# Image 0 in four quarters, its tables from a second queue, and unread products on TensorE ahead of the first statistics

## The reference, cut to what matters

```python
def _gn(v, G=32, eps=1e-05):
    g = v.reshape(B_, H_, W_, G, C_ // G)
    m = jnp.mean(g, axis=(1, 2, 4), keepdims=True)
    s = jnp.var(g, axis=(1, 2, 4), keepdims=True)
    return ((g - m) / jnp.sqrt(s + eps)).reshape(v.shape)

def _L0_conv_ref(x, w1, b1, w2, b2, bias_w, bias_b):
    bias = x @ bias_w.T + bias_b
    xf = jnp.fft.rfftn(x.reshape(B, H, W, 4, 96), axes=(1, 2), norm='ortho')
    xr, xi = (xf.real, xf.imag)
    r1 = relu(_block_mul(xr, w1[0]) - _block_mul(xi, w1[1]) + b1[0])
    i1 = relu(_block_mul(xr, w1[1]) + _block_mul(xi, w1[0]) + b1[1])
    r2 = _block_mul(r1, w2[0]) - _block_mul(i1, w2[1]) + b2[0]
    i2 = _block_mul(r2, w2[1]) + _block_mul(i1, w2[0]) + b2[1]
    out = jnp.fft.irfftn(complex(r2, i2), s=(H, W), axes=(1, 2), norm='ortho')
    return out.reshape(B, H, W, C) + bias

return x + _L0_conv_ref(_gn(x), ...)
```

## Time and profile before

| | us |
|---|---|
| median of 3 runs | 426.53 (425.56 to 427.38) |
| the profiled execution's own time | 424.55 |
| its span | 422.7 |
| TensorE busy | 392.5 (93%) |
| VectorE busy | 289.6 (68%) |
| ScalarE busy | 228.7 (54%) |
| mean granted TensorE clock | 0.984 |

### The profile page before, as it was taken

The page is one execution under the profiler, slowest core; times in us unless marked ns, Lnnn a source line. Parts: engine busy times, 40 slices in busy tenths (PEclk is TensorE's granted clock), DMA queues, the critical chain, the costliest instruction groups (busy, mean ns, idle before and its releaser), DMA issues.

```text
span 422.7 us, 19391 instructions
## 1 busy us (share of the span) xinstructions
PE 392.5 (93%) x8578; PEld 323.9 (77%) x8578; DVE 289.6 (68%) x728; ACT 228.7 (54%) x514; POOL 167.5 (40%) x114
## 2 busy tenths in 40 slices
PE   3369799999999999999999999999999999998996
PEld 3367689887887878788787878788787988876794
DVE  4797677874687557865678657865578747877525
ACT  2884766356752676447662667436663567426420
POOL 0000001990049600992039800793019900699200
PEclk9859999999999999999999999999999999999999
DMA  6670000180003500170002600062001800040004
GB/s 219 184 256 4 2 3 4 40 299 3 3 17 147 182 3 4 40 283 20 3 4 105 236 3 5 29 227 86 3 5 40 301 3 3 18 174 3 5 3 151
DMA packets 12407, 32.98 MB, mean 78 GB/s; under 512 B 4962, under 2 KB 6660, under 8 KB 12324
## 3 DMA queue, kind: packets, MB, share of 16 engines
q1 hardware_dynamic: 12324, 31.74, 21.2%
HBM read 16.00 MB, written 12.58 MB: 68 GB/s over the span
## 4 chain that ended last, share of the span: by engine, by line
PE 86%; ACT 5%; DVE 4%; issue 2%; DMA 1%; DVEq 0%; SPq 0%; ACTq 0%
PE bank L576 86%; DVE rho L1047 2%; DMA x_sb<-in_x 1%; ACT rho L969 1%; ACT y L930 1%; ACT junk L918 1%; ACT yraw L910 1%; ACT r L940 1%; ACT biasw L944 1%; DVE o_sb L1142 0%; ACT w2s L944 0%; DVE r L1126 0%; ACT z L950 0%; ACT junk L921 0%; DVE w1R L1047 0%
## 5 line engine op out<-in xcount | busy, mean ns | idle before, releaser
L576 PE MATMUL bank<-biasw,yt 128*64 128x384 f16 x1008 | 92.6, 327 | 0.0
L576 PE MATMUL bank<-w2s,rho 128*64 128x96 f16 x3072 | 84.9, 207 | 0.0
L882 POOL TENSOR_TENSOR x_sb<-x_sb,added 128x384 f32<-128x384 f32 x8 | 8.0, 1001 | 192.1 <-DVE yraw L1113 192.1
L576 PEld LDWEIGHTS bank<-w2s,rho 128*64 128x64 f16 x3072 | 80.0, 109 | 5.3 <-issue 2.5
L892 POOL COPY yt<-y 128x1024 f16<-128x1024 f16 x42 | 84.1, 2059 | 0.0
L884 POOL TENSOR_TENSOR x_sb<-x_sb,added 128x384 f32<-128x384 f32 x56 | 74.6, 1364 | 0.0
L576 PEld LDWEIGHTS bank<-biasw,yt 128*64 128x64 f16 x1008 | 54.0, 110 | 20.2 <-issue 0.3
L576 PE MATMUL bank<-w1R,y 128*128 128x192 f16 (+3 forms) x768 | 60.3, 228 | 5.4 <-ACT y L930 3.4
L1047 DVE SCALAR_TENSOR_TENSOR rho<-bank,rho 128x256 f16<-128x256 f32 (+2 forms) x128 | 40.2, 365 | 32.1 <-ACT rho L969 18.6
L950 ACT ACTIVATE z<-bank 128x384 f16<-128x384 f32 x72 | 35.3, 490 | 49.0 <-PE bank L576 48.1
L576 PE MATMUL bank<-tab,x_sb 128*128 128x128 f32 x384 | 50.5, 287 | 8.1 <-DMA x_sb<-in_x 6.5
(11 more groups left out here) (116 smaller groups left out, 474.6 us busy)
## 6 DMA issues: line engine op xcount, KB each, us to landing
x_sb<-in_x SPq DMA_DIRECT2D x16, 768.0 KB, 7.2
out<-o_sb SPq DMA_DIRECT2D x14, 768.0 KB, 4.0
y<-y SPq DMA_DIRECT2D x24, 128.0 KB, 2.7
out<-o_sb SPq DMA_DIRECT2D x8, 192.0 KB, 1.9
tab<-in_tab SPq DMA_DIRECT2D x1, 672.0 KB, 6.3
o_sb<-in_bias_wt SPq DMA_DIRECT2D x4, 144.0 KB, 2.8
b1raw<-in_b1h SPq DMA_DIRECT2D x1, 384.0 KB, 6.6
g<-in_w2t SPq DMA_DIRECT2D x2, 144.0 KB, 2.6
```

The source lines that it names most:

```text
L576: return nc.tensor.matmul(o, lhsT, rhs, start=start, stop=stop, **kw)
L882: nc.gpsimd.tensor_tensor(tiles[:, 0, :], tiles[:, 0, :], added[:, 0, :], ALU.add).then_inc(x_shifted, 1)
```

## The change

- SP issues x of image 0 as four transfers of two tiles each, with a semaphore each (x0_loaded), as its first instructions; the width table is issued by ACT as ACT's first instruction. p1 of image 0 waits for a quarter ahead of the matmuls that use it.
- TensorE gets three batches of products that nobody reads: b1ones as weights, and b1ones repeated four times as 512 columns, into the bank c_bank[2]. Ten stand after p1(0), behind a wait for b1ones; seven after mean(0); twelve after the w2 products, before c1.
- The high part of the first third of y of image 0 is made by DVE (first_high) instead of ACT; ACT makes the second and third.
- largest_bias moves behind the three y_low on DVE.
- The counts of x_loaded for image 2 and later even images change, as image 0 no longer counts there.

```diff
@@ SP
-            sp.dma_start(tab[:, 0:WIDTH_COLS], tab_d[:, 0:WIDTH_COLS]).then_inc(width_in, 16)
-            load(0, 0)
+            for q in range(4):
+                sp.dma_start(x_sb[0][:, 2 * q:2 * q + 2, :].rearrange("p t c -> p (t c)"),
+                             x[0, :, q * 2 * CH:(q + 1) * 2 * CH]).then_inc(x0_loaded[q], 16)
@@ TensorE, p1
-                if ct == 0:
-                    pe.wait_ge(x_loaded[p][h], (b - p) * 8 + 16)
+                if ct == 0 and not first:
+                    pe.wait_ge(x_loaded[p][h], (b - p) * 8 + 16 * p)
                 for i in range(4):
                     t = 4 * h + i
+                    if first and ct == 0 and i % 2 == 0:
+                        pe.wait_ge(x0_loaded[t // 2], 16)
@@ TensorE, opening
+            def idle_products(n):
+                ones = b1ones[:, :].rearrange("k (o n) -> k o n", o=1).to_broadcast([128, 4, 128])
+                for _ in range(n):
+                    mm(c_bank[2][:, 0:512].rearrange("k (o n) -> k o n", o=4), b1ones[:, :], ones, True, True)
             for m in range(Y_ITEMS):
                 p1(0, 0, m, first=True)
+            pe.wait_ge(b1_ready, 5)
+            idle_products(10)
             pe.wait_ge(consts_in, 16)
             mean(0)
+            idle_products(7)
             variance(0)
...
             last.then_inc(w2_prod, 1)
+            idle_products(12)
             image(0, 0, first=True)
@@ ACT
-            def y_high(b, p, ct):
+            def y_high(b, p, ct, tiles=1):
...
+            nc.scalar.dma_start(tab[:, 0:WIDTH_COLS], tab_d[:, 0:WIDTH_COLS]).then_inc(width_in, 16)
             act.wait_ge(zeroed, N_ZERO)
...
-            for ct in range(NT):
-                y_high(0, 0, ct)
+            y_high(0, 0, 1, tiles=2)
+            y_high(0, 0, 2)
@@ DVE
-                dve.wait_ge(yh_ready, NT * b + ct + 1)
+                if b == 0 and ct == 0:
+                    dve.wait_ge(first_high, 1)
+                else:
+                    dve.wait_ge(yh_ready, NT * b + ct + 1)
...
             scales(0)
-            largest_bias()
+            dve.wait_ge(dve_step, CENTRED)
+            nc.vector.tensor_scalar(y[0][:, 0, 0, :, :], yraw[:, 0, :, :], rstd[:, 0:1], None, ALU.mult).then_inc(first_high, 1)
             for ct in range(NT):
                 y_low(0, 0, ct)
+            largest_bias()
             second_forms()
```

More of the change, by code:

```diff
@@ L338, in spectral_block_kernel @@
         x_loaded = [[sem(f"x_loaded{p}{h}") for h in range(2)] for p in range(2)]
+        x0_loaded = [sem(f"x0_loaded{q}") for q in range(4)]
         width_in = sem("width_in")
@@ L378, in spectral_block_kernel @@
         yl_ready = sem("yl_ready")
+        first_high = sem("first_high")
         yt_ready = sem("yt_ready")
@@ L926, in std @@
                 nc.scalar.activation(std_t[:, :], var[:, :], ACT.Sqrt).then_inc(std_ready, 1)
-            def y_high(b, p, ct):
+            def y_high(b, p, ct, tiles=1):
                 act.wait_ge(dve_step, NSTEP * b + CENTRED)
-                nc.scalar.activation(y[p][:, 0, ct, :, :], yraw[:, ct, :, :], ACT.Copy, scale=rstd[:, ct:ct + 1]).then_inc(yh_ready, 1)
+                nc.scalar.activation(y[p][:, 0, ct, :, :], yraw[:, ct, :, :], ACT.Copy, scale=rstd[:, ct:ct + 1]).then_inc(yh_ready, tiles)
             def g_high(b, gi, more):
```

## The result

The changed kernel took 422.76 us (median of 13 runs, 421.18 to 425.0) against 425.84 (424.63 to 428.02, 13 runs): ratio 0.9925, 95% interval 0.9907 to 0.9943. The profiled execution took 422.8 against 424.55, span 421.0 against 422.7.

What follows compares the result with a forecast made beforehand. TensorE is dense from 63.75 us, so the gain lies before 40 us, where it waits on small DVE and ACT steps. 426.53 - 1.62 - 0.5 = 424.4 us, range 422.8 to 426.4.

Steps and rivals of the forecast that it cites:

- Quarters, SP's order, statistics, y: Opening of image 0: p1 gains 1.2 us, moments starts 1.05 earlier, c1's wait ends near 26.1 instead of 27.87.
- Unread products: TensorE's gaps before c1: 0.22 us each at 2.4 GHz, at no cost, their only gain being cover against slow clock.
- rival 3: Before c1: clock falls in the gaps, products get in the way, 1.4 us slower, 427.9; chance 0.12.
- a warm clock buys nothing once DVE binds: c1 to z of unit 3: DVE ends at 34.4, TensorE at 32.75 warm or 34.3 cold, so DVE is the bound.
- p3_half(0) 1.62 us earlier: End of the opening: 1.05 us from earlier statistics plus 0.57 from DVE's idle time going, so p3_half(0) near 36.8.
- what comes behind is the same work: After p3_half(0): TensorE's later work is unchanged, so the end moves by the opening's 1.62 us.
- The 2.0 us between profile and median: Profile 424.55 against median 426.53: possibly longer half-clock time in p1 and c1, half in each place.
- the 0.5 us that the sum took for it: Opening, c1: half of the 1.0 us of extra half-clock time in the median that might fall away.
- Rival 2: Opening: the clock rises late in the median execution, so more is covered, giving 423.3; chance 0.20.

Runs made afterwards that it cites:

- e15: The changed kernel timed once more, nothing altered: 423.18 us, ratio 0.9938 to the kernel before.
- e5: The changed kernel with its unread products cut from 512 columns to 4: 422.52 us, ratio 0.9928 to the kernel before.
- e1: The kernel before with only the 29 unread products of 512 columns added: 423.22 us, ratio 0.9956.
- e8: The kernel before with only 29 unread products added, of 4 columns instead of 512: 425.11 us, ratio 0.9977.
- e4: The changed kernel without the unread products: 424.92 us, ratio 0.9989 to the kernel before.
- e0: The kernel before timed again, nothing altered: 425.44 us, ratio 0.9997; its profiled execution took 425.78.
- e2: The kernel before with only the quarters of x and the width table on ACT's queue: 425.35 us, ratio 1.0004.
- e3: The kernel before with only first_high on DVE and largest_bias moved: 425.69 us, ratio 1.0003.
- e6: The changed kernel with the three shift loads issued ahead of tab16 and b1 on SP: 423.76 us, ratio 0.9952.

## Why the prediction was wrong

- *Quarters, SP's order, statistics, y*: right. p1 started at 4.92 (4.8 forecast) and ended at 12.88 (12.9); first_scale began at 11.28 (11.2) and was, as named, what is late next: the 0.74 wait is gone; moments 17.99 (18.15), high 0 0.75 (0.75), c1 25.99 (26.1). p1's releaser was width, on ACT's queue, 4.1 us after its issue (2.2 alone on SP's): the two transfers did share the engines.
- *Unread products*: right in size at full clock (2.32 for ten, 0.23 each) and in cost, nothing. They do not always hold the clock: in e15, after idle times of 2.16 and 1.55 us, it stood at 0.50 from 22 to 24 us, and the twelve took 4.15 us instead of 2.76 and ended only as c1 began, at 26.12. That is part of the condition of rival 3 without its price: c1 starts 8.01 us after moments there and 8.00 in the first profile, so the twelve did not hold it up. That a warm clock buys nothing once DVE binds is shown by e5, whose c1 ran at 0.50 and whose p3_half(0) stood at 36.85; e1 against e8 shows 1.9 us in the opening where DVE does not bind.
- *p3_half(0) 1.62 us earlier*: 0.87 in the first profile of the changed kernel, 1.54 in its second (e15). The term left out is bias_all: SP's shift of 0.43 was carried to the tables and w2, not to the landing of the last shift load. Before, ACT reached b2row at 26.95 with no wait; with the changed list of SP bias_all let it start at 26.35 (e5), 27.55 (e15) and 28.23 (first profile). Only with the last was p3_half(0) late, so the landing spreads by more than the shift.
- **The step that failed** is "what comes behind is the same work". It was the same work at another place in TensorE's program, and the wait for code there fell: images 1, 3 and 5 together from 147.17 to 145.96 in the two profiles, and e4 to e5 by 2.4 us in the medians. The trace of before held the sign: stalls of 0.85, 0.56 and 0.55 put down to "issue" in one place of every second image.
- *The 2.0 us between profile and median* were laid on the clock. e0 shows the same clock at 425.78, with a longer stall, and e5 shows that the clock was not what the changed kernel gained. So the 0.5 us that the sum took for it stands for nothing that the runs show. The sum also began at 426.53, the median of three runs; from the 425.84 of thirteen the same terms give 423.7, 0.9 above the result. That the miss was not larger is in part luck: the 0.5 made up for some of what the shorter stalls gave, which the sum lacked. Rival 2 had nearly the size (423.3), by a mechanism that the runs refute.

What stays open: why the stall of one kernel is 0.55 in one execution and 1.43 in another, why loads alone lengthen it, and why tiny products are worth 2.4 us in the changed kernel and nothing clear of the noise in the kernel before. What the share of the opening in the 3.1 us is, no run tells: e2, e3 and e4 open 0.6 to 1.0 earlier than before, and none of their medians is clear of no change.

## What to carry to other kernels

A gap put down to "issue" that returns at the same count of instructions can be a wait for code: look at what fills the DMA engines ahead of it, and split that transfer with a release early enough for its own reader. Before crediting added instructions with what they are for, run them empty. When a queue's issues are moved back, follow the shift to the last one that somebody waits for.

## What the runs showed that was not expected

No instruction packet of 16 KB passed until a store and an x load, 3 MB together, were nearly through; they kept the DMA engines at 0.94 busy from 84.5 to 93 us. TensorE's idle time for it was 0.3 to 1.75 us, and behind the longest, in e6, the granted clock fell to 0.50 in the dense stretch. Holding one half of the x load back was worth 3.1 us, as much as the whole change.
